# Front pieces of a group four steps nearer its batches, a second gauge buffer, last linear rows stored by ScalarE, and weights, keys and sums on GpSimd

## Time and profile before

| | |
|---|---|
| median of 3 runs | 694.59 us |
| the profiled execution | 695.72 us, its span 693.9 us |
| busy in the span | TensorE 370.7, VectorE 496.9, ScalarE 373.2, GpSimd 228.7 us |
| alignment, to its last row | to 216.25 us |
| first `nearest` (step -2), of step 0, of step 28 | 256.06, 265.09, 426.08 us |
| first expert matmul | 449.03 us |

### The profile page before, as it was taken

The page is one execution under the profiler, slowest core; times in us unless marked ns, Lnnn a source line. Parts: engine busy times, 40 slices in busy tenths (PEclk is TensorE's granted clock), DMA queues, the critical chain, the costliest instruction groups (busy, mean ns, idle before and its releaser), DMA issues.

```text
span 693.9 us, 13468 instructions
## 1 busy us (share of the span) xinstructions
PE 370.7 (53%) x3107; PEld 305.2 (44%) x3108; DVE 496.9 (72%) x1773; ACT 373.2 (54%) x1106; POOL 228.7 (33%) x430
## 2 busy tenths in 40 slices
PE   0400000000000127777767887789999999999930
PEld 0200000000000015555655665678888888888830
DVE  1969999999994578888988977876744444444425
ACT  0434444444442129998977989554455455544510
POOL 1035454545453000000004332465675333333320
PEclk9999999999999998988889979999999999999975
DMA  5177804040324332333250000122332111111129
GB/s 105 45 177 172 178 9 96 4 92 7 88 57 95 106 120 63 108 98 86 74 159 32 23 24 20 53 59 60 81 95 65 41 45 42 45 43 45 39 82 283
DMA packets 113096, 54.06 MB, mean 78 GB/s; under 512 B 56988, under 2 KB 108828, under 8 KB 112947
## 3 DMA queue, kind: packets, MB, share of 16 engines
q1 hardware_dynamic: 106478, 44.53, 26.4%
q0 software_dynamic: 4320, 8.47, 3.7%
q10 hardware_dynamic: 2237, 0.38, 0.4%
HBM read 29.61 MB, written 24.19 MB: 78 GB/s over the span
## 4 chain that ended last, share of the span: by engine, by line
DVE 34%; PE 34%; ACT 13%; issue 8%; DMA 7%; SPq 3%; ACTq 0%; DVEq 0%; POOLq 0%
PE ps L752 9%; PE ps L569 5%; DVE D L1196 5%; DVE D L1205 5%; PE ps L571 5%; PE ps L570 5%; PE ps L742 4%; DVE ps L1185 3%; ACT ps L851 3%; ACT D L857 3%; ACT sq L942 3%; DMA gb<-g_dram 3%; DVE mn L1365 2%; ACT sq L935 2%; DMA iota_sb<-in_iota 2%
## 5 line engine op out<-in xcount | busy, mean ns | idle before, releaser
L1087 POOL DMA_INDIRECT xd_dram<-pay,slot x64 | 62.2, 972 | 212.6 <-DVE pay L1444 185.4
L1108 POOL DMA_INDIRECT y_dram<-ybuf,dest x71 | 69.8, 983 | 100.1 <-DVE ybuf L1550 85.1
L1528 DVE TENSOR_TENSOR sq<-sq,ps 128x512 f32<-128x512 f32 x71 | 48.8, 688 | 70.1 <-PE ps L571 54.6
L605 PE MATMUL ps<-zdiag,ones_f 32*128 32x32 f32 x2 | 0.6, 408 | 181.3 <-DVE zdiag L1273 181.3
L1064 POOL TENSOR_TENSOR D<-D 128x128 f32<-128x128 f32 x130 | 56.2, 432 | 119.2 <-DVE D L1219 59.6
L990 ACT ACTIVATE sq<-ps 128x512 f32<-128x512 f32 x71 | 42.5, 598 | 75.7 <-PE ps L571 75.7
L857 ACT ACTIVATE D<-D 64x2 f32<-64x2 f32 (+1 forms) x154 | 31.3, 204 | 94.6 <-DVE D L1205 78.5
L605 PEld LDWEIGHTS ps<-zdiag,ones_f 32*128 32x128 f32 x2 | 0.5, 308 | 181.4 <-DVE zdiag L1273 181.4
L942 ACT ACTIVATE sq<-sq,mn 128x128 f32<-128x128 f32 x256 | 78.2, 397 | 0.0
L752 PE MATMUL ps<-wdn,xnt 128*128 x568 | 76.2, 277 | 1.9 <-issue 1.2
L752 PEld LDWEIGHTS ps<-wdn,xnt 128*128 128x128 f32 x568 | 69.0, 192 | 4.7 <-issue 4.7
(11 more groups left out here) (222 smaller groups left out, 1062.3 us busy)
## 6 DMA issues: line engine op xcount, KB each, us to landing
stage<-xd_dram SPq DMA_DIRECT2D x71, 65.0 KB
D<-th_dram SPq DMA_DIRECT2D x16, 208.0 KB, 4.0
g_dram<-D SPq DMA_DIRECT2D x14, 208.0 KB, 4.2
x_dram<-D SPq DMA_DIRECT2D x14, 208.0 KB, 4.4
h0q<-g_dram SPq DMA_DIRECT2D x8, 256.0 KB, 3.0
gb<-g_dram SPq DMA_DIRECT2D x8, 256.0 KB, 3.6
xf<-x_dram SPq DMA_DIRECT2D x8, 256.0 KB, 3.2
xb<-x_dram SPq DMA_DIRECT2D x8, 256.0 KB, 3.9
```

The lines of the kernel that those rows point to most:

```text
L1087: pool.indirect_dma_start(xd_dram, bass.IndirectOffsetOnAxis(slot[:, q, j, k:k + 1], 0), pay[q % 3][:, k, j, :], None).then_inc(s_sc[2 * k ...
L1108: pool.indirect_dma_start(y_dram, bass.IndirectOffsetOnAxis(dest[:, w:w + 1], 0), yrow[w], None, bounds_check=2 * NB * T - 1, oob_is_err=F ...
```

## The change

The diff moves the pieces of a quad's front (from the gauge load to the keys) to later steps: most by four, `first_norms` from 9 to 5 ahead, `turn_tokens` from 8 to 5, `queries_keys` from 4 to 3. In the back `normalise` goes from step 4q+6 to 4q+5 and `gate_logits` to 4q+12 for all quads. `gb` and `hs` get two buffers, so a gauge load waits for the quad before the last one. The linear half of the last two pieces of rows (6 of the 12 stores) is issued by ScalarE, ahead of its logarithm of the total. GpSimd takes over the high and low parts of the weights, the keys of the heads (`kx`), the normed sum `h1` and the second copy of the payload; the scatters of a quad go two a step, over four steps, instead of four a step over two. In the diff's text, a name in brackets says which function a line is in.

```diff
-        gb = sb("gb", [T, 4, T])
+        gb = [sb(f"gb{k}", [T, 4, T]) for k in range(2)]
-        hs = sb("hs", [128, 2, 4])
+        hs = sb("hs", [128, 2, 2, 4])
...
+        def store_rows(eng, c, first, end, gauge=True, linear=True):
...
+                    if gauge:
+                        eng.dma_start(lane_rows(g_dram, d, h, lo, hi), rows).then_inc(s_lst[c], 16)
+                    if linear:
+                        eng.dma_start(lane_rows(x_dram, d, h, lo, hi),
+                                      X[lanes, at:at + hi - lo, 1:H + 1]).then_inc(s_lst[c], 16)
...
-                store_rows(BLKS - 1, first, end)
+                store_rows(sp, BLKS - 1, first, end, linear=(first < LAST[2]))
...
             def load_gauge(q):
+                need(sp, s_xn, q - 1)
                 need(sp, s_hx, q - 1)
-                need(sp, s_e2, q)
+                need(sp, s_e2, q - 1)
...
-                quad(load_linear, n, 14)
-                quad(load_gauge, n, 17)
+                quad(load_linear, n, 10)
+                quad(load_gauge, n, 13)
...
-                need(pe, s_x3t, q - 4)                       (turn_tokens)
+                need(pe, s_x3t, q - 3)
...
+                need(pe, s_rkc, q - 4)                       (project)
...
-                pe.wait_ge(s_qk, q + 1)                      (distances)
+                pe.wait_ge(s_kx, q + 1)
...
-                quad(turn_tokens, n, 8)
+                quad(turn_tokens, n, 5)
                 quad(spread, n, -5)
-                late(gate_logits, n, -13, 1)
+                quad(gate_logits, n, -12)
                 quad(merge, n, -6)
                 quad(turn_inputs, n, -10)
-                quad(project, n, 5)
+                quad(project, n, 4)
...
+            act.wait_ge(s_lin, STEPS - SKEW)
+            store_rows(act, BLKS - 1, LAST[2], LAST[3], gauge=False)
+            act.wait_ge(s_lin, STEPS)
+            store_rows(act, BLKS - 1, LAST[3], LAST[4], gauge=False)
             act.wait_ge(s_zm, 2)
...
                 pair(square, n, 2)
-                quad(qk_high, n, 4)
+                quad(root_first, n, 5)
+                quad(qk_high, n, 3)
+                quad(tokens_high, n, 4)
                 pair(exponentials, n, 1)
                 pair(turned, n, 0)
                 quad(numerators, n, -4)
                 quad(root_second, n, -8)
-                quad(tokens_high, n, 7)
-                quad(copy_inputs, n, -10)
                 quad(inputs, n, -11)
-                quad(root_first, n, 10)
-                quad(posterior, n, 13)
+                quad(posterior, n, 9)
                 quad(values, n, 2)
                 quad(gates, n, -15)
-                if 0 <= n + 1 < CHUNKS:
-                    weights_high(n + 1)
...
+            def inputs_normed(q):
+                pool.wait_ge(s_hs, q + 1)
+                for k in range(4):
+                    m = pool.tensor_scalar(h1[:, 4 * q + k, :], h0q[q % 2][:, k, :], hs[:, q % 2, 0, k:k + 1],
+                                           hs[:, q % 2, 1, k:k + 1], ALU.mult, ALU.add)
+                m.then_inc(s_hx, 1)
+            def weights(c):
+                hi, lo, staged = parts_of(c)
+                pool.wait_ge(s_stage[c % 2], 16 * (c // 2 + 1))
+                pool.tensor_copy(hi, staged).then_inc(s_whi, 1)
+                pool.wait_ge(s_whi, c + 1)
+                pool.tensor_tensor(lo, staged, hi.bitcast(f32), ALU.subtract).then_inc(s_wlo, 1)
+            def keys_of_heads(q):
+                pool.wait_ge(s_qk, q + 1)
+                need(pool, s_d, 4 * q - 4)
+                pool.tensor_tensor(kx[q % 2][:].rearrange("p (h s) -> p h s", s=T), each(qk_k[:], NH),
+                                   over(mask_sb[:], T), ALU.mult).then_inc(s_kx, 1)
+            def copy_inputs(q):
+                pool.wait_ge(s_x3, q + 1)
+                pool.tensor_copy(pay[q % 3][:, :, 1, 0:E], pay[q % 3][:, :, 0, 0:E]).then_inc(s_x3c, 1)
...
-                quad(sent, n, -18)
-                quad(send_two, n, -16)
-                quad(send_others, n, -17)
+                quad(sent, n, -20)
+                quad(keys_of_heads, n, 3)
+                quad(copy_inputs, n, -10)
+                quad(inputs_normed, n, 5)
+                if n >= 16 and (n - 16) // 4 < NQ:
+                    send((n - 16) // 4, n % 4)
+                if 0 <= n + 1 < CHUNKS:
+                    weights(n + 1)
...
                 pair(nearest, n, 2)
-                quad(normalise, n, -6)
                 late(read_ranks, n, -16, 1)
-                quad(queries_keys, n, 4)
+                quad(queries_keys, n, 3)
                 quad(residual, n, -7)
                 late(second_moments, n, -7, -1)
-                quad(log_posterior, n, 15)
                 pair(turned, n, 0)
+                quad(normalise, n, -5)
                 quad(second_norms, n, -9)
                 late(choose_first, n, -14, 1)
                 quad(choose_second, n, -14)
-                quad(first_norms, n, 9)
-                quad(posterior, n, 11)
-                quad(first_moments, n, 10)
+                quad(first_norms, n, 5)
+                quad(posterior, n, 8)
+                quad(log_posterior, n, 11)
+                quad(first_moments, n, 6)
                 quad(denominators, n, -4)
                 late(places, n, -16, 1)
                 quad(gate_weights, n, -16)
-                if 0 <= n < CHUNKS:
-                    weights_low(n)
```

More of the change, by code:

```diff
@@ L268, in tower @@
         s_consts = sem("s_consts")
-        s_ldq = sem("s_ldq")
+        s_ldq = [sem(f"s_ldq{k}") for k in range(2)]
         s_half = sem("s_half")
@@ L428, in sent_rows, with over, each @@
             return 16 * (k // YR + 1) if isinstance(k, int) else k - w + 16
+        def over(a, n):
+            return bass.AP(tensor=a.tensor, offset=a.offset, ap=[a.ap[0], a.ap[1], [0, n]])
+        def each(a, n):
+            return bass.AP(tensor=a.tensor, offset=a.offset, ap=[a.ap[0], [0, n], a.ap[1]])
+        def store_rows(eng, c, first, end, gauge=True, linear=True):
+            for h in range(2):
+                lo, hi = span(c, h)
+                lo, hi = max(lo, c * ROWS + first), min(hi, c * ROWS + end)
+                if lo >= hi:
+                    continue
+                at = slot_of(c, lo - c * ROWS + 1)
+                for d in range(2):
+                    lanes = slice(64 * h + 32 * d, 64 * h + 32 * d + 32)
+                    rows = M[lanes, at:at + hi - lo, 1:H + 1] if d else N[lanes, lo % RING:lo % RING + hi - lo, :]
+                    if gauge:
[3 more added lines that the diff above has]
+                                      X[lanes, at:at + hi - lo, 1:H + 1]).then_inc(s_lst[c], 16)
         CHUNKS = 2 * NX
@@ L455, in _ @@
                                      lane_rows(th_dram, d, h, lo, hi)).then_inc(s_th[c], 16)
[L457 to L470, removed]
             for c in range(BLKS - 1):
                 sp.wait_ge(s_lin, ROWS * (c + 1))
-                store_rows(c, 0, ROWS)
+                store_rows(sp, c, 0, ROWS)
             for first, end in zip(LAST, LAST[1:]):
                 sp.wait_ge(s_lin, STEPS - ROWS + end)
-                store_rows(BLKS - 1, first, end)
+                store_rows(sp, BLKS - 1, first, end, linear=(first < LAST[2]))
             for c in range(BLKS):
@@ L619, in project @@
                 need(pe, s_msk, q - 4)
+                need(pe, s_rkc, q - 4)
                 for k in range(4):
@@ L1337, in first_norms @@
                 inverse_roots(0, 2)
-                V_.tensor_scalar(hs[:, 0, :], r1[:, 0, 0, :], 1.0, None, ALU.add)
-                link(V_.scalar_tensor_tensor(hs[:, 1, :], mv[:, 0, :, 0], -1.0, r1[:, 0, 0, :], ALU.mult, ALU.mult))
+                need(dve, s_hx, q - 1)
+                V_.tensor_scalar(hs[:, q % 2, 0, :], r1[:, 0, 0, :], 1.0, None, ALU.add)
+                V_.scalar_tensor_tensor(hs[:, q % 2, 1, :], mv[:, 0, :, 0], -1.0, r1[:, 0, 0, :], ALU.mult, ALU.mult).then_inc(s_hs, 1)
                 need(dve, s_va, q - 1)
@@ L1345, in first_norms @@
                 m.then_inc(s_xn, 1)
-                for k in range(4):
-                    m = V_.tensor_scalar(h1[:, 4 * q + k, :], h[:, k, :], hs[:, 0, k:k + 1], hs[:, 1, k:k + 1],
-                                         ALU.mult, ALU.add)
-                m.then_inc(s_hx, 1)
             def queries_keys(q):
@@ L1357, in queries_keys @@
                 V_.tensor_scalar(qs[q % 2][:], qk_x[:], rowc_sb[:, 1:2], rowc_sb[:, 2:3], ALU.mult, ALU.add)
-                link(V_.tensor_scalar(qk_k[:], qk_x[:], rowc_sb[:, 3:4], rowc_sb[:, 4:5], ALU.mult, ALU.add))
-                V_.tensor_tensor(kx[q % 2][:].rearrange("p (h s) -> p h s", s=T), each(qk_k[:], NH),
-                                 over(mask_sb[:], T), ALU.mult).then_inc(s_qk, 1)
+                need(dve, s_kx, q)
```

(1 more changed line is left out.)

50 lines of the change are left out of this document (15 added, 35 removed).

## The result

The changed kernel takes **718.88 us** (median of 4 runs, 717.77 to 719.56) against 694.54 for the kernel before beside it: ratio 1.0345, 95% interval 1.0326 to 1.0364. It is slower by 24 us; the forecast was 696.6, in 685 to 705. The profiled span grew from 693.9 to 715.9 us, by 22.0.

The account below looks back on a forecast made before the run. No engine was full throughout the attention loop, so the prediction followed dependences up to the first expert matmul, with TensorE setting the time from there. Prologue -15.7, loop +16.7, tail +1.1 gave +2.1 us: 696.6, range 685 to 705.

Parts of the forecast that it names:

- Prologue: Start, up to step 0's nearest: split stores and nearer front bring it to 249.4 from 265.09, a gain of 15.7 us.
- first-call rule: Prologue, GpSimd: a freshly loaded routine's first call costs about 6 us more; by it nearest(0) would come at 243.4.
- branch (b): Prologue after xn: transposes, projection, query/key operations, keys on GpSimd, distances and square put nearest(0) at 240.5, later than gauge 2's path.
- same-step wait r3 to r0: From a quad's fourth step to the next quad's first: transposes of the same step's xn precede distances; VectorE stands 3.0 us.
- The quads: Attention loop in groups of four steps: seven quads sum to 177.7 us against 161.0 before, a loss of 16.7.
- some 17 us of VectorE: Loop: keys, h1 and weight remainders taken from VectorE, less one front's 6 us, save some 17 us of its time.
- costed at nothing: Loop: the gauge load, earlier gate_logits, GpSimd's weights and the payload buffer were given no cost.
- rival A: Loop, second and third steps of quads: TensorE's lower clock adds 1.2 us a quad, +8, 705; chance 0.35 together with C.
- From there TensorE sets the time and nothing of that loop changes: Expert tiles, from the first expert matmul at 449.03: TensorE sets the time, so only that matmul's shift counts.
- Tail: Step 28's nearest to first expert matmul: 24.0 us against 22.95, for later places and a payload copy among the sends.
- B: Loop: same-step waits are shorter, some 9 to 11 us in all, giving 687.5; chance 0.25.
- C: Prologue: scalar-queue stores bring nothing, or h1 on GpSimd sets nearest(0); +1.5 to +3, 698 to 699.6; chance 0.35 together with A.

Follow-up runs that it names:

- e3: Changed kernel with first norms, first moments and what precedes them one step earlier, so xn is made a step before turn_tokens: 705.90 us, ratio 1.0146.
- e10: Kernel before with one number changed, turn_tokens nine steps ahead instead of eight, in the step that makes its xn: 715.11 us, ratio 1.0291.
- e4: Changed kernel with all four GpSimd moves undone (weights, keys, h1, payload copy); offsets, stores and second gauge buffer as changed: 713.24 us, ratio 1.0252.
- e18: Changed kernel with normalise of the last quad alone put at the head of the next step: 710.44 us, ratio 1.0235.
- e7: Kernel before with only the second gauge buffer and the last linear rows stored by ScalarE, on a chip where the kernel before took some 753 us: ratio 0.9970.
- e12: Kernel before with only the second gauge buffer and the last linear rows stored by ScalarE: 693.17 us, ratio 0.9973.

## Why the prediction was wrong, step by step

**Prologue: right.** First nearest at 240.5 forecast, 240.63 measured; step 0's at 249.4 against 249.76; gain 15.7 against 15.3. GpSimd's prices: keys 1.89 (2.2 taken), h1 3.00 at its first call and 1.94 in the loop row at 319.2 (1.5 taken). The 6 us of the first-call rule did not appear: the first h1 began 0.1 us after its factors. The terms of branch (b) add up to 240.3, not 240.5.

**The same-step wait r3 to r0: right in mechanism, and nearly in size.** "VectorE stands 3.0" measured 3.4 to 3.5 at the end of six of the seven quads; the seventh, without a front, has 1.9. This wait is the largest cause of the loss: without it 12.6 of the loop's 25.4 us come back (e3), and it alone costs the old order 17.0 (e10). The idle time before the reciprocal was forecast at 1.7 and measured at 1.56.

**The quads: mis-sized, 8.7 us.** Forecast 22.3, 25.2, 25.7, 26.3, 27.8, 27.8, 22.6; measured 22.4, 25.8, 25.7, 30.1, 30.0, 28.5, 24.1. One term is that of VectorE's time: "some 17 us of VectorE" less was taken at full worth, as if its other instructions kept their length. Its busy time in the loop fell by 3.8 us (137.1 to 133.3). Between the kernels with and without the moves in the same order (e4) the saving on VectorE was 26.0 us and the stretching 13.5. At step 13 it sets the time: the forecast has 1.35 us idle in such a step of a full quad, measured are 3.7 us of stretching and no idle time (9.61 us for 7.35). Elsewhere it is not in step with the miss. Summed over each quad as the excess over e4's durations, it is 3.2 us in the first, which was forecast to 0.1 us, and 0.8 and 0.2 in those of steps 16 to 23, which were missed by 2.2 and 0.7.

For steps 16 to 19 the trace shows other terms. From nearest to nearest the forecast has 6.25, 7.35, 5.4 and 8.8 us, and the changed kernel 7.30, 8.10, 5.36 and 9.24:

```profile
356.25 1.88 PE L715 MATMUL ps<-wg_sb,x3t 128*128 128x8 f32 x8
358.64 1.22 PE L646 MATMUL ps<-kx,qs 32*128 32x512 f32 x2
360.95 1.22 DVE L1384 TENSOR_REDUCE mn<-sq 128x8 f32<-128x1024 f32 x1 [1.00 <-ACT sq L953]
364.94 0.69 DVE L1399 TENSOR_TENSOR ont<-ont,ps 128x512 f32<-128x512 f32 x1 [1.28 <-PE ps L689]
```

VectorE ends places when forecast, but then stands 1.00 us, because the distances come behind `gate_logits` (L715), which the diff moved into this step and the forecast "costed at nothing"; in the step after, normalise stands 1.28 us for the spread of the same step. TensorE's work is slow there (gate_logits 1.88 us, 0.96 in the kernel before), which is rival A's mechanism (0.68 to 0.78 granted). No run separates the order of these pieces from the clock; that share stays open.

**"From there TensorE sets the time and nothing of that loop changes. So the change is worth what it does to 449.03": wrong, 9.5 us.** The diff moves normalise from the head of one step into the step of its spread, and the last of them stands at step 33, between tiles 0 and 1, ahead of column_low. The forecast followed normalise in the loop but ended its path at the first expert matmul. e18 takes back 5.4 us of this in the gap and 8.4 in the total.

**Tail: nearly right**, 24.0 forecast, 25.3 measured. In all the profiled execution misses its forecast by 19.9 us (0.4, 8.7, 1.3 and 9.5); the medians miss by 22.3, because the profile before was 1.1 us above its median and the profile after 1.1 below.

**The rivals.** A (slower by TensorE's clock, 705) had the sign. Its places are in the trace: the wait of r3 is 0.4 to 0.5 us longer than forecast, and normalise waits 1.28 and 1.61 us at steps 17 and 21, where A had 0.7. Its 8 us are near the 8.7 by which the quads were missed, but stretching, which A did not have, is part of these, and the 9.5 us in the tiles are none of it. B and C did not come. The slower side had 0.35, and the range ended 14 us short, because the forecast and its rivals had no price for stretching or for the handover to the tiles: the only mention of longer VectorE instructions was in the list of what would show the forecast wrong, without a price.

## What to carry to other kernels

When a schedule written in steps is shifted, write down for every consumer whether its producer now stands in the same step: on an engine with an ordered queue such a wait holds everything behind it, and one number was worth 20 us here (e10), more than all that the shift gained. Work given to GpSimd is not free for VectorE: price it with the lengthening of VectorE's instructions that read two SBUF operands, a half to three quarters of what was given away here (13.5 and 19.4 of 26.0 us in two traces of one loop). And follow a moved piece to its last instance, where it may stand in front of the first work of the next stage.

## What the hardware showed unexpectedly

GpSimd's work stretched single VectorE instructions on SBUF from 0.34 to as much as 1.61 us (log_posterior) and a four-element-wide step from 0.16 to 0.88, while nearest (1.22) and the copies out of PSUM (0.68) kept their length. The kernel before took 694 to 695 us beside most of the runs and 753 beside the other two lots, each lot on a chip of its own. Between one program's traces on the two kinds of chip, 15 of 20 quads up to step 20 agree within 0.3 us (e7 and e12: 20.45 and 20.45, 23.02 and 23.02), though the sums differ by up to 2.9 us; the difference in the total is made of stops behind that, mostly in the expert tiles (e7 takes 285.0 us from the first expert matmul to the end, e12 245.7).
